# Gate products of a slot-routing layer: three split products in twelve weight pieces instead of one fp32 product, and one pass over all slots instead of two

## The reference, cut to what matters

```
xn = layernorm(x)
h = gelu(concat(xn, slot_mean) @ w1 + b1); route = (h @ w2 + b2) / (|tau| + 0.1)
alpha = softmax over the 8 largest of 64 slots, zero elsewhere    # [8, 512, 64]
si = (alpha^T @ xn) / sum(alpha)                                  # [8, 64, 512]
i_r, i_z, i_n = split(si @ Wih.T + bih, 3)                        # the gate products
h_r, h_z, h_n = split(S @ Whh.T + bhh, 3)                         # S = slot_init
r = sigmoid(i_r + h_r); z = sigmoid(i_z + h_z); n = tanh(i_n + r * h_n)
S_new = (1 - z) * n + z * S
attn = softmax((S_new @ wq + bq) @ (S_new @ wk + bk)^T / sqrt(128))
y = layernorm(S_new + attn @ (S_new @ wv + bv))
out = x + (alpha @ (y @ wvp + bvp)) @ wo + bo
```

## Time and profile before

| | before |
|---|---|
| median of three runs | 363.48 us |
| profiled execution, and its span | 363.83 us, 362.0 us |
| busy PE / DVE / POOL / ACT | 348.7 / 253.3 / 188.9 / 186.8 us |
| gate products: L1404 x96, L1674 x96 records | 32.3 us, 10.9 us |
| chain that ended last | PE 72%, DVE 11%, POOL 6% |

### The profile page before, as it was taken

One profiled execution on the slowest core, in us unless ns is written; L12 is line 12 of the kernel. 1 busy time (PEld: TensorE's weight loads), 2 busy tenths in 40 slices (PEclk: granted clock), 3 DMA queues, 4 the chain that ended last, 5 costly groups with the idle time before them and its releaser, 6 DMA issues.

```text
span 362.0 us, 6908 instructions
## 1 busy us (share of the span) xinstructions
PE 348.7 (96%) x2260; PEld 276.1 (76%) x2260; DVE 253.3 (70%) x729; ACT 186.8 (52%) x384; POOL 188.9 (52%) x340
## 2 busy tenths in 40 slices
PE   8999999999999999999999999999999999999991
PEld 5475648999997988898898988977556696676660
DVE  5367886877788787787886786666583334768774
ACT  2440125568659577677587586487262126422341
POOL 5053057888776876686677677541011112342693
PEclk9999999999999999999999999999999999999997
DMA  7799866243232322313314100039200000002399
GB/s 282 229 362 343 308 178 194 61 117 92 85 113 64 96 82 58 118 60 90 87 62 115 32 0 4 0 101 363 97 1 0 2 0 0 3 0 87 147 348 348
DMA packets 40934, 42.78 MB, mean 118 GB/s; under 512 B 3246, under 2 KB 32046, under 8 KB 40899
## 3 DMA queue, kind: packets, MB, share of 16 engines
q1 hardware_dynamic: 39088, 40.41, 33.8%
q10 hardware_dynamic: 1522, 1.27, 1.1%
q0 software_dynamic: 288, 0.66, 0.6%
HBM read 32.18 MB, written 8.39 MB: 112 GB/s over the span
## 4 chain that ended last, share of the span: by engine, by line
PE 72%; DVE 11%; POOL 6%; issue 4%; ACT 3%; DMA 2%; DVEq 0%; SPq 0%; POOLq 0%; ACTq 0%
PE psum L349 12%; PE psum L350 11%; PE psum L351 11%; PE psum L1404 9%; PE psum L1454 5%; PE psum L1300 4%; PE psum L1674 3%; PE psum L1482 3%; PE psum L1342 2%; PE psum L1698 2%; PE psum L1435 2%; PE psum L1600 2%; POOL X L492 2%; PE psum L1517 1%; POOL hT_lo L487 1%
## 5 line engine op out<-in xcount | busy, mean ns | idle before, releaser
L349 PE MATMUL psum<-GW_hi,hT_hi 128*128 128x292 f32 (+1 forms) x256 | 78.9, 308 | 1.1 <-POOL GW_lo L474 1.0
L351 PE MATMUL psum<-GW_lo,hT_hi 128*128 128x292 f32 (+1 forms) x256 | 74.0, 289 | 0.0
L350 PE MATMUL psum<-GW_hi,hT_lo 128*128 128x292 f32 (+1 forms) x256 | 73.9, 289 | 0.0
L492 POOL TENSOR_TENSOR X<-X,th 128x512 f32<-128x512 f32 x32 | 38.3, 1196 | 31.5 <-ACT th L1098 31.5
L349 PEld LDWEIGHTS psum<-GW_hi,hT_hi 128*128 128x128 f32 x256 | 48.5, 189 | 2.9 <-issue 2.0
L487 POOL TENSOR_TENSOR hT_lo<-xT,hT_hi 128x512 fp32r<-128x512 f32 x32 | 43.4, 1356 | 13.7 <-ACT hT_hi L1054 13.7
L350 PEld LDWEIGHTS psum<-GW_hi,hT_lo 128*128 128x128 f32 x256 | 48.3, 189 | 0.2 <-issue 0.2
L351 PEld LDWEIGHTS psum<-GW_lo,hT_hi 128*128 128x128 f32 x256 | 48.1, 188 | 0.0
L349 PE MATMUL psum<-xhT_hi,w_hi 128*128 128x256 f32 x128 | 38.4, 300 | 0.1
L350 PE MATMUL psum<-xhT_hi,w_lo 128*128 128x256 f32 x128 | 36.1, 282 | 0.0
L351 PE MATMUL psum<-xhT_lo,w_hi 128*128 128x256 f32 x128 | 36.0, 282 | 0.0
(11 more groups left out here) (263 smaller groups left out, 827.7 us busy)
## 6 DMA issues: line engine op xcount, KB each, us to landing
X<-in_x SPq DMA_DIRECT2D x32, 256.0 KB, 3.5
xT<-in_xT SPq DMA_DIRECT2D x32, 256.0 KB, 2.8
out<-ost SPq DMA_DIRECT2D x32, 256.0 KB, 2.7
WhhT<-in_WhhT SPq DMA_DIRECT2D x1, 3072.0 KB, 13.1
WihT<-in_WihT SPq DMA_DIRECT2D x4, 768.0 KB, 8.6
Wo<-in_wo ACTq DMA_DIRECT2D x4, 256.0 KB, 4.8
WvpT<-in_WvpT SPq DMA_DIRECT2D x4, 256.0 KB, 5.6
WaT<-in_WaT SPq DMA_DIRECT2D x1, 1024.0 KB, 11.1
```

Source lines behind the costliest of these rows:

```text
L349: pe.matmul(out, w_hi, m_hi, start=start, stop=False)
L350: pe.matmul(out, w_lo, m_hi, start=False, stop=False)
L351: return pe.matmul(out, w_hi, m_lo, start=False, stop=stop)
L492: pool.tensor_tensor(tile_x(r), tile_x(r), halves(th[:, :]), ALU.add).then_inc(S("x2"), 1)
```

## The change

Gate products. `siT` becomes two tiles, `siT_hi` (written by ACT) and `siT_lo` (written by DVE from the PSUM bank, `low_slot_sums(b)`), for every batch. `WihT` is cast piece by piece into twelve tiles `W_hi[c, gate]` of [128, 4, 128] by DVE (`high_piece_of`), and POOL writes the low half over `WihT` in place (`low_piece`; `W_lo` lies on `WihT`). The pieces of chunk 0 and one of chunk 1 lie on space that is free early; the others on `xhT`, free when the first layer is done. Every gate product is `mm3`. Chunk 0 is done for the first 384 slots, interleaved with the routing of batches 6 and 7, and for the last 128 slots when batch 7 is in; chunks 1 to 3 are done for all 512 slots, on two sets of three banks in turn. `late_gate` and its elementwise work go; the elementwise work of each chunk is over 512 columns. The gates run in the order r, n, z. Keys and queries are one product each over 512 columns, begun on chunks 0 to 2 while chunk 3 is finished. The four score blocks are one group on PE and two pairs after it, and `weights_turned` takes pairs.

Moved: the bias product (L1719) from after the keys to after gate (1, 0); `turned_slots` in ACT's loop from the end of a step to ahead of `tanh_of`; the load of `blockmask` behind a wait for the logits of batch 7, since it now lies on `lgT`; POOL's order of `low_Wp` and ACT's of `high_Wp`; the orders of the output stage on DVE, ACT, POOL and PE.

```diff
-        def early_gate(c, gate):
-            i = 3 * c + gate
-            pe.wait_ge(S(f"in_wih{c}"), 16)
...
-                last = pe.matmul(RING[gate][:, 0:EN], WihT[:, k, i * P:(i + 1) * P], siT[:, k, 0:EN],
-                                 start=k == 0, stop=k == KC - 1)
-            last.then_inc(S("gi"), 1)
+        def gate_sum(c, gate, lo, hi):
+            n = PIECES.index((c, gate))
+            pe.wait_ge(S("wlo"), n + 1)
...
+                if c > 1:
+                    pe.wait_ge(S(("gr_in", "gz_in", "gn_in")[gate]), c - 1)
             for k in range(KC):
+                last = mm3(pe, RINGS[c % 2][gate][:, lo:hi], W_hi[c, gate][:, k, :], W_lo[:, k, w_piece(c, gate)],
+                           siT_hi[:, k, lo:hi], siT_lo[:, k, lo:hi], k == 0, k == KC - 1)
+            if hi == SLOTS:
+                last.then_inc(S("gi"), 1)
...
+        gate_sum(0, 0, 0, EN)
+        logits(7)
         for q in range(TPB):
             slot_sums(6, q)
         turn_logits(7)
+        gate_sum(0, 2, 0, EN)
+        turn_slots(6, TURN, 2)
+        gate_sum(0, 1, 0, EN)
         for q in range(TPB):
             slot_sums(7, q)
+        turn_alpha(5, trX, 0)
+        turn_slots(7, TURN, 2)
+        pe.wait_ge(S("te"), EP)
+        turn_alpha(7, trX, 0)
+        pe.wait_ge(S("siv"), 2 * NB)
+        for gate in RUN_GATES:
+            gate_sum(0, gate, EN, SLOTS)
+        gate_sum(1, 0, 0, SLOTS)
+        pe.wait_ge(S("bp"), 1 + KC)
+        pe.matmul(TURN, ones[:, :], rows[:, :], start=True, stop=True).then_inc(S("bp_all"), 1)
...
+        for c in range(2, KC):
+            for gate in RUN_GATES:
+                gate_sum(c, gate, 0, SLOTS)
...
+        pe.wait_ge(S("snt"), KC - 1)
+        product_of(Wq, banks[0], 0, KC - 1)
+        product_of(Wk, banks[1], 0, KC - 1)
         pe.wait_ge(S("snt"), KC)
+        product_of(Wk, banks[1], KC - 1, KC)
+        y_slots(0)
+        product_of(Wq, banks[0], KC - 1, KC)
...
# DVE, end of the loop
+        low_slot_sums(4, TURN)
         slot_inputs(5)
+        high_piece_of(0)
+        high_piece_of(1)
         logits_out(6)
         low_xh(30)
         low_xh(31)
+        low_slot_sums(5, TURN)
         topk(6, 0)
         topk(6, 1)
         topk(6, 2)
+        for n in range(2, 6):
+            high_piece_of(n)
         slot_inputs(6)
+        logits_out(7)
...
+        low_slot_sums(6, TURN)
+        slot_inputs(7)
+        for n in range(6, len(PIECES)):
+            high_piece_of(n)
+        low_slot_sums(7, TURN)
         for c in range(KC):
             v.wait_ge(S("bp"), c + 1)
             v.scalar_tensor_tensor(rows[:, :], Wp[:, c, :], lnb[:, c:c + 1], rows[:, :], ALU.mult, ALU.add).then_inc(S("bp"), 1)
...
# POOL
+        def low_piece(n):
+            c, gate = PIECES[n]
+            pool.wait_ge(S("whi"), n + 1)
+            pool.tensor_tensor(W_lo[:, :, w_piece(c, gate)], WihT[:, :, w_piece(c, gate)], W_hi[c, gate][:, :, :].bitcast(F32),
+                               ALU.subtract).then_inc(S("wlo"), 1)
...
         def low_Wp(c):
             pool.wait_ge(S("wp"), 2 * KC + c + 1)
...
+        low_Wp(3)
+        low_Wp(1)
         low_Wp(0)
+        scales_y(0)
+        low_alpha(0)
         low_Wp(2)
...
+        low_alpha(2)
+        low_slot_values(1)
         out(5)
...
# ACT, behind the gates (high_Wp(c) raises "wp" by one, from 8)
+        high_alpha(0)
+        high_Wp(3)
+        gate(last, 1)
+        high_Wp(0)
+        high_values_weight()
+        act.wait_ge(S("snt"), KC)
         high_slots(V1, EN)
+        key()
         high_slots(EN, SLOTS)
+        query()
         high_Wp(1)
+        exps(0, 2, 1)
+        exps(2, 4, 2)
         high_Wp(2)
+        high_alpha(1)
         high_y(0)
```

More of the change, by code:

```diff
@@ L105, in program, with high_piece @@
     bvr = place("bvr", [P, D], F32, "b1")
-    blockmask = place("blockmask", [P, P], F32, "b1")
+    W_hi = {}
+    def high_piece(c, gate, where):
+        W_hi[c, gate] = place(f"W_hi{c}{gate}", [P, KC, P], F32R, where)
+    region("b6", cursor["b1"])
+    high_piece(0, 0, "b1")
+    high_piece(0, 2, "b1")
+    bpb = place("bpb", [P, D], F32, "b6")
     V1, VN = P, SLOTS - P
@@ L193, in program @@
     ost = [place(f"ost{i}", [P, D], F32, "c4") for i in range(4, 8)]
-    siT = place("siT", [P, KC, SLOTS], F32, "keep")
+    siT_lo = place("siT_lo", [P, KC, SLOTS], F32R, "keep")
     ghT = place("ghT", [P, GC, NS], F32, "keep")
@@ L210, in program @@
     madd = place("madd", [P, NB * WS], F32, "keep")
+    region("bm", cursor["keep"])
+    blockmask = place("blockmask", [P, P], F32, "bm")
     lgT = place("lgT", [P, HT], F32, "keep")
@@ L342, in bc, with gate_done, w_piece @@
         return ap.unsqueeze(axis).broadcast_to(shape[:axis] + [n] + shape[axis:])
-    def late(buf):
-        return buf[:, 0, :].rearrange("p (c b s) -> p c b s", c=KC, s=NS)
+    def gate_done(c, gate):
+        return 3 * c + 1 + RUN_GATES.index(gate)
+    def w_piece(c, gate):
+        return slice((3 * c + gate) * P, (3 * c + gate + 1) * P)
+    PIECES = [(c, gate) for c in range(KC) for gate in RUN_GATES]
     def mm3(pe, out, w_hi, w_lo, m_hi, m_lo, start, stop):
@@ L825, in step @@
                 weights_of(s)
+            for b in range(NB):
+                if SLOT_STEP[b] + TPB == s:
+                    low_slot_sums(b, trX)
             if live(s + 3):
@@ L861, in _, with scores @@
             v.scalar_tensor_tensor(rows[:, :], Wp[:, c, :], lnb[:, c:c + 1], rows[:, :], ALU.mult, ALU.add).then_inc(S("bp"), 1)
[L862 to L873, removed]
+        for c in range(KC):
             gate_in(c, 0)
+            candidate_own(c)
+            candidate_in(c)
             gate_in(c, 1)
-            candidate_in(c)
             new_slots(c)
-        l4 = lambda a: a.rearrange("p (c b s) -> p c b s", c=KC, s=NS)
         s3 = lambda a: a.rearrange("p (g n) -> p g n", n=P)
[L882 to L908, removed]
+        def scores(lo, hi):
+            v.wait_ge(S("ss"), 1)
             link(v.scalar_tensor_tensor(sc[:, lo:hi, :], s3(SB)[:, lo:hi, :], float(DQ) ** -0.5,
@@ L1134, in step @@
                 norm2(s - 2)
+            for b in range(NB):
+                if SLOT_STEP[b] + TPB == s:
+                    turned_slots(b, trX)
             if live(s - 1):
@@ L1169, in _ @@
         gelu(7, 1)
-        gate(0, 0)
-        gate(0, 1)
         logits_biased(7)
-        turned_alpha(5, TURN)
+        exp_top(7)
+        turned_slots(6, TURN)
+        turned_alpha(5, trX)
+        turned_slots(7, TURN)
+        turned_alpha(7, trX)
         act.wait_ge(S("bp"), 1 + KC)
@@ L1461, in turn_alpha, with turn_slots @@
             last.then_inc(S("tt"), 1)
-        def turn_slots(b, bank):
+        def turn_slots(b, bank, pairs=None):
             pe.wait_ge(S("sin"), b + 1)
-            wait(pe, S("siv"), b)
-            wait(pe, S("te"), b // 2)
+            wait(pe, S("siv"), 2 * b)
+            wait(pe, S("te"), b // 2 if pairs is None else pairs)
             for k in range(2):
@@ L1669, in values_of @@
             last.then_inc(S("sv_mm"), 1)
-        def late_gate(gate):
-            for c in range(KC):
-                for k in range(KC):
-                    last = pe.matmul(LATE[gate][:, c * LN:(c + 1) * LN], WihT[:, k, (3 * c + gate) * P:(3 * c + gate + 1) * P],
-                                     siT[:, k, EN:], start=k == 0, stop=k == KC - 1)
-            last.then_inc(S("gi_late"), 1)
         def outs(m):
@@ L1741, in _ @@
         outs(0)
-        values(3, 2, KC)
-        y_turned(1)
-        y_slots(3)
         outs(1)
-        outs(2)
+        values_of(1)
         y_of(3)
         y_turned(2)
-        values_of(1)
+        outs(2)
         outs(3)
         values_of(2)
-        outs(4)
         y_turned(3)
-        for m in (5, 6, 7, 8):
+        for m in (4, 5, 6, 7):
             outs(m)
         values_of(3)
-        for m in range(9, NT // 2):
+        for m in range(8, NT // 2):
             outs(m)
```

321 lines of the change are left out of this document (145 added, 176 removed).

## The result

The changed kernel takes 370.79 us (median of four runs, 370.24 to 372.75), the kernel before 363.88 us beside it (four runs, 363.45 to 364.46). The ratio is 1.0199, 95% interval 1.0155 to 1.0242: slower, as forecast, but 5.8 us above the 365.0 and 1.3 us above the range. The profiled execution took 372.75 us, the highest of the four; its span is 371.0 us.

The account below looks back on a forecast made before the run. PE, busy 348.7 of 362.0 us, was taken as the bound. Terms from -7.1 (gate products) to +6.4 (a wait) summed to +1.5 us: 365.3 us profiled, 365.0 as median, 8-in-10 range 360.0 to 369.5.

Parts of the forecast that it names:

- Gate products, -7.1: PE's gate products: split products take 35.3 us in place of 42.4, 7.1 less (3.0 to 8.9 by the bounds).
- 0.9 for the bias product: Gate stage on PE: the bias product moves in from the next stage, 0.9 us here, 0 in the whole sum.
- Start and routing, +0.4 and +0.9: Before batch 7's wait: two casts delay the first gate product by 0.4 us; batch 7's top-8 and transposes cost 0.9.
- Wait for batch 7's low half, +6.4: PE idles 6.4 us while six DVE casts, alternating with POOL's differences on shared ports, precede the low half.
- PE's clock, +0.3: Behind the 6.4 us wait PE's clock falls, but short pieces run first, so only 0.3 us is lost.
- Keys to slot values, +1.8 at y: PE waits 1.8 us at `y_turned(0)`, as y's scale stands behind POOL's late low halves of Wp (0 to 3).
- Output stage, -0.5: Output stage: same work in another order, `high_y(3)` and `low_y(3)` before they are needed; 0.5 us less.
- Slow short products: Rival: 36 short fp32r gate products at the upper bound, +4.1 us, 369.1 us; chance 0.2 with blocking, 0.08 without.
- DVE keeps the ports: Rival: queued DVE casts shut POOL out, 4.5 us of the wait go, clock stays up; 360.2 us, chance 0.2.
- The queue of outputs decides: Rival: DVE's and POOL's output work and DMA swallow PE's gain or loss; 363.5 us, no change, chance 0.12.

Follow-up runs that it names:

- e1: The changed kernel with batch 7's low half moved ahead of the last six weight casts on DVE; 367.5 us, ratio 1.0077.
- e3: The changed kernel with 24 extra matmuls of 128 columns filling PE's idle time ahead of its wait for batch 7's low half; 365.67 us, ratio 1.0032.
- e5: As e1, with the four bias rows also ahead of the six casts on DVE; 362.26 us, ratio 0.993.
- e2: The changed kernel with POOL's last six differences held until batch 7's low half is done; 366.34 us, in three groups of runs.
- e4: The changed kernel with ACT's and POOL's output-stage orders put nearer to those before, tile 5 earlier; 372.57 us, ratio 1.0215.
- e6: As e5, with POOL making y's first scale right behind `low_Wp(3)`; 360.69 us, ratio 0.9887.
- e7: As e5, with the last six weight casts made by ACT, not DVE; 362.11 us, ratio 0.9909.
- e9: As e5, with Wp's halves made in the order 0, 1, 2, 3 on ACT and POOL, y's first scale after them; 363.73 us, ratio 0.997.
- e10: As e9, with the last six weight casts made by ACT as in e7; 360.97 us, ratio 0.9893.

## Why the prediction was wrong, step by step

- **Gate products, -7.1: right.** 36 short products are 0.11 us apart at 2.4 GHz (e1, e3), those of 512 columns 0.231. In e5, where nothing waits for long, keys begin 4.1 us sooner than before; the prediction's terms for that case (-7.1 + 0.4 + 0.9 + 0.5 of wait + 0.9 for the bias product) give -4.4.
- **Start and routing, +0.4 and +0.9: right in sum.** The first gate product begins 5.7 us after the copy in both kernels, so nothing was lost at the start. PE's last transposes end 19.7 us after the copy (265.67 - 245.93); forecast were 265.3 - 245.35, 20.0.
- **Wait for batch 7's low half, +6.4: right.** PE resumes 25.5 us after the copy; forecast 271.7 - 245.35 = 26.4. The wait itself is 5.74 us. The six casts took 6.37 us, forecast 6.7. e2 shows the cause, e5 against e3 the price up to the keys (5.3 us).
- **PE's clock, +0.3: the step that failed.** It is the term of the sum that was mis-sized: 5.9 us between e3 and the changed kernel at the begin of the keys. The prediction saw the fall and took it that, as the short pieces run first, little would be slowed. Both halves of that are wrong. A short piece at 1.2 GHz takes 0.214 us, not 0.11; it isn't bound by a fixed cost. And the clock did not come back while they ran: it stayed low for 12.7 us of uninterrupted work, until 12 pieces of 512 columns had been slowed as well, for which the text had had "some 2 us" and left it out. With e3, the same kernel without this term, the measured difference is +0.32% or 1.2 us (0.1 to 2.3 us by the interval); the prediction without it says +1.2. That the two agree to a tenth is luck, as the interval and the misses of single terms show.
  The 5.9 us hold for the profiled execution, whose mean clock is 0.966. The other three have 0.973 and 0.974, so by an estimate (0.0075 x 371/0.5) the clock was low for 5 to 6 us less in them, in which of the two falls isn't shown; and the medians of the changed kernel and e3 are 5.1 us apart. In e4, with the same wait, PE needs 35.3 us from its return to the keys, in the changed kernel 35.9, in e3 30.0: the loss was 5.3 and 6.0 us.
- **Keys to slot values, +1.8 at y: right in kind.** PE waited for 1.29 us there, behind POOL's `low_Wp(3)`, as forecast; but e6 shows that the term can't be taken out by itself.
- **Output stage, -0.5: wrong, cause open.** From the start of the keys to the end of the span the kernel before takes 62.4 us, e3 61.7, the changed kernel 63.7. In the changed kernel PE waits for output tiles for 2.2 us and the clock falls a second time. The chain of waits of the kernel after runs through one output transfer:

```profile
351.80 4.60 DMA out<-ost
```

  It lasts 4.60 us where the median of the page is 3.1. But this isn't a matter of that one execution: e1, e5, e6 and e7 take 63.4 to 63.6 us for the same stretch, without a fall of the clock there while PE works. Why e3 is 2 us shorter no run shows. Of the gap of the medians, 6.9 us, the clock (5.1 by the medians, 5.9 by the traces) and the rest of the sum (1.2 by e3) account for 6.3 to 7.1.
- **Rivals.** Slow short products: refuted by e1 and e3 (they are slow at the low clock only). DVE keeps the ports: refuted by 6.37 us. Its price was too low as well: it assumed that a wait of 1.9 us leaves the clock up, and in e2, behind one of 1.47 us, the clock was down. The queue of outputs decides: not the cause of the loss, but it takes part of what is gained (e5).

## What to carry to other kernels

An idle stretch of PE has two prices: the wait, and the work behind it at half clock, which in the changed kernel cost as much again (5.74 us and 5.3 to 6.0), and three times as much in e2 (1.47 us and 4.7). When a sum contains a new wait on PE, add the work that stands behind it at about twice its cost, for the 5 to 13 us that the low clock lasted here after PE resumed, and look whether cheap matmuls can fill it. A change of DVE's order moves every result behind it too: list who waits for each (the bias rows in e1), and treat DVE and POOL as one engine wherever both work from SBUF (the casts, the bias rows, the new slots).

## What the hardware showed that I had not expected

- The clock stayed at 1.2 GHz long after PE had resumed work: 12.7 us in the changed kernel, 10.0 us in e2, 5.0 us in e1, with waits of 5.74, 1.47 and 4.25 us before them. In e9, behind a wait of 2.51 us, it fell only 1.4 us after PE had resumed, and came back 3.4 us later. What sets the length was not tested.
- The length of a wait doesn't tell by itself whether the clock falls. A wait of 1.47 us in e2 had a fall with it, and one of 1.48 us for an output tile in the changed kernel. Waits of 1.48 and 1.49 us for an output tile had none in e7, e1 and e10, nor had the 1.29 us before the y transposes in the changed kernel.
- Split products with 128 columns take twice as long at half clock (0.214 against 0.112 us), and the records of their weight loads last 0.33 us (changed kernel) in place of 0.19 us (e3).
